# Retrieval scores on one core: the first loads are issued behind single gathers of tile 0

## The reference, cut to what matters

```
retrieved = mean(item_embeddings[indices], axis=1)      # 512 users x 50 indices -> 512 x 512
fused     = concat([user_rep, retrieved], 1) @ W_fuse + b_fuse      # (512 x 1024) @ (1024 x 512)
logits    = fused @ W_proj + b_proj                     # (512 x 512) @ (512 x 12500)
```

## Time and profile before

| What | Value |
|---|---|
| Median of 3 runs | 305.21 us (304.76, 305.21 and 759.52) |
| The profiled execution | 304.97 us, of it the span 303.1 us |
| PE busy | 293.3 us (97%) |
| DVE busy | 241.8 us (80%) |
| ACT busy | 159.4 us (53%) |
| POOL busy | 73.2 us (24%) |
| TensorE's mean granted clock | 0.999 |
| DMA over the span | 75.14 MB, mean 248 GB/s |

### The profile page before, as it was taken

One profiled execution on the slowest core, in us unless ns is written; L12 is line 12 of the kernel. 1 busy time (PEld: TensorE's weight loads), 2 busy tenths in 40 slices (PEclk: granted clock), 3 DMA queues, 4 the chain that ended last, 5 costly groups with the idle time before them and its releaser, 6 DMA issues.

```text
span 303.1 us, 4065 instructions
## 1 busy us (share of the span) xinstructions
PE 293.3 (97%) x1371; PEld 240.0 (79%) x1371; DVE 241.8 (80%) x349; ACT 159.4 (53%) x216; POOL 73.2 (24%) x76
## 2 busy tenths in 40 slices
PE   3999999999999999999999999999999999999995
PEld 1559887978888888888778888888888888888884
DVE  5888999668668699769998979979799797995133
ACT  1205666533544558967465675556855568453310
POOL 4766786777777100000000000000000000000000
PEclk9999999999999999999999999999999999999999
DMA  7999999896997247557875939749397493442315
GB/s 250 363 386 372 402 389 360 297 368 200 333 376 254 71 140 221 185 162 310 292 285 174 352 118 309 286 152 349 123 306 282 143 367 122 152 155 107 128 70 203
DMA packets 32480, 75.14 MB, mean 248 GB/s; under 512 B 4445, under 2 KB 20587, under 8 KB 32460
## 3 DMA queue, kind: packets, MB, share of 16 engines
q1 hardware_dynamic: 25340, 58.31, 54.6%
q0 software_dynamic: 5536, 13.73, 13.2%
q10 hardware_dynamic: 1584, 2.84, 2.5%
HBM read 52.84 MB, written 25.60 MB: 259 GB/s over the span
## 4 chain that ended last, share of the span: by engine, by line
PE 48%; DVE 3%; issue 1%; ACT 0%; DVEq 0%; ACTq 0%
PE pair L1258 16%; PE pair L1256 16%; PE pair L1259 16%; DVE w_lo L962 1%; DVE part_out L987 0%; DVE out_sb L987 0%; DVE w_raw L953 0%; DVE t_sums L945 0%; ACT odd_sum L644 0%; DVE out_sb L1119 0%; DVE t_sums L951 0%; DVE t_sums L957 0%; DVEq L983 0%; DVEq L956 0%; ACTq L639 0%
## 5 line engine op out<-in xcount | busy, mean ns | idle before, releaser
L438 POOL DMA_INDIRECT ring<-item_embeddings,rows x56 | 59.1, 1055 | 19.6 <-issue 15.2
L1256 PE MATMUL pair<-w_hi,s_hi 128*128 128x500 f32 x144 | 56.2, 390 | 0.4 <-ACT odd_sum L644 0.3
L1258 PE MATMUL pair<-w_lo,s_hi 128*128 128x500 f32 x144 | 56.1, 389 | 0.0
L1259 PE MATMUL pair<-w_hi,s_lo 128*128 128x500 f32 x144 | 55.9, 388 | 0.0
L1183 PE MATMUL pair<-w_hi,f_hi 128*128 128x500 f32 x112 | 44.0, 393 | 0.4 <-DVE f_lo L895 0.4
L854 DVE SCALAR_TENSOR_TENSOR pair<-ring,mask,pair 128x512 f32<-128x512 f32 x48 | 36.2, 753 | 9.8 <-DMA ring<-item_embeddings,rows 5.5
L1183 PE MATMUL pair<-w_lo,f_hi 128*128 128x500 f32 x112 | 43.8, 391 | 0.0
L1183 PE MATMUL pair<-w_hi,f_lo 128*128 128x500 f32 x112 | 43.5, 389 | 0.0
L1258 PE MATMUL pair<-w_lo,f_hi 128*128 128x500 f32 x108 | 42.2, 391 | 0.0
L1259 PE MATMUL pair<-w_hi,f_lo 128*128 128x500 f32 x108 | 42.0, 389 | 0.0
L1256 PE MATMUL pair<-w_hi,f_hi 128*128 128x500 f32 x108 | 41.8, 387 | 0.0
(11 more groups left out here) (137 smaller groups left out, 431.2 us busy)
## 6 DMA issues: line engine op xcount, KB each, us to landing
w_raw<-w_proj SPq DMA_DIRECT2D x28, 500.0 KB, 7.5
logits<-part_out SPq DMA_DIRECT2D x24, 500.0 KB, 3.2
early<-w_proj SPq DMA_DIRECT2D x22, 500.0 KB, 5.9
logits<-out_sb SPq DMA_DIRECT2D x23, 250.0 KB, 2.5
logits<-out_sb SPq DMA_DIRECT2D x11, 500.0 KB, 3.2
first_bias<-b_proj SPq DMA_DIRECT2D x10, 250.0 KB, 6.4
s_sum<-b_proj SPq DMA_DIRECT2D x8, 250.0 KB, 7.0
logits<-out_sb ACTq DMA_DIRECT2D x7, 250.0 KB, 7.0
```

Of the source, the lines that this page charges most:

```text
L438: return nc.gpsimd.indirect_dma_start(out=to, out_offset=None, in_=table, in_offset=bass.IndirectOffsetOnAxis(ap=column, axis=0), **how)
L1256: nc.tensor.matmul(ps[:, q, 0:CHUNK], f, hi, start=start and k == 0, stop=False, skip_group_check=True)
L1258: nc.tensor.matmul(ps[:, q, 0:CHUNK], f, lo, start=False, stop=False, skip_group_check=True)
L1259: m = nc.tensor.matmul(ps[:, q, 0:CHUNK], f_rest, hi, start=False, stop=stop and k == 1, skip_group_check=True)
```

## The change

The second half of the user part (k = 2 and 3) is no longer loaded at the start: `user_t[:, 2]` and `wf_user[:, 2]` are issued by SP once slot 0 of tile 0 has landed, those of k = 3 once slot 2 has. ACT now issues only `user_t` of k = 0 and 1. The first half of chunk 0 waits for slot 3, the last row (and the bias rows and `bf_col` behind it) for slot 4, the second half of chunk 0 for slot 5, `wf_ret` for slot 6, chunk 1 for slot 8. `wf_ret` now comes ahead of chunk 1. Chunks 2 to 6 wait for `user_fused` as before, and for slot 8 instead of slot 7.

```diff
-GATE = 7
+USER_BEHIND = (0, 2)
+GATE = 8
...
-            def load_chunk(c):
-                for h in range(2):
+            def load_chunk(c, halves=(0, 1)):
+                for h in halves:
...
             sp.dma_start(idx[:, 0:K], indices[:, 0:K]).then_inc(first_idx_landed, 16)
+            def behind_slot(i):
+                sp.wait_ge(slot_landed[place(0, i)], 16 * slot_uses(0, i))
+
             for k in range(HK):
+                if k >= HK // 2:
+                    behind_slot(USER_BEHIND[k - HK // 2])
+                    sp.dma_start(user_t[:, k, :], user_dram[k]).then_inc(user_landed[k], 16)
                 sp.dma_start(wf_user[:, k, :], wf_dram[0, :, k, :]).then_inc(wf_user_landed[k], 16)
                 if k == 0:
                     sp.dma_start(idx[:, K:TILES * K], indices[:, K:TILES * K]).then_inc(idx_landed, 16)
+            behind_slot(3)
+            load_chunk(0, (0,))
+            behind_slot(4)
             sp.dma_start(last_rows[:], last_item.to_broadcast([P, H])).then_inc(last_landed, 16)
-            load_chunk(0)
             sp.wait_ge(total_zeroed, 1)
             for row in (0, LO_ROW):
                 sp.dma_start(bias_rows[row:row + RESIDENT, :],
                              b_proj[0:RESIDENT * CHUNK].rearrange("(c n) -> c n", n=CHUNK))\
                   .then_inc(bias_rows_landed, 16)
             sp.dma_start(bf_col[:], b_fuse).then_inc(bf_landed, 16)
+            behind_slot(5)
+            load_chunk(0, (1,))
+            behind_slot(6)
+            sp.dma_start(wf_ret[:], wf_dram[1]).then_inc(wf_ret_landed, 16)
+            behind_slot(8)
             load_chunk(1)
-            sp.dma_start(wf_ret[:], wf_dram[1]).then_inc(wf_ret_landed, 16)
             sp.wait_ge(user_fused, 1)
-            sp.wait_ge(slot_landed[place(0, GATE)], 16 * slot_uses(0, GATE))
+            behind_slot(GATE)
             for c in range(2, RESIDENT):
                 load_chunk(c)
...
-            for k in range(HK):
+            for k in range(HK // 2):
                 act.dma_start(user_t[:, k, :], user_dram[k]).then_inc(user_landed[k], 16)
```

## The result

The changed kernel takes 313.76 us (median of 4 runs, 311.88 to 313.84) against 305.25 us: 1.027 times as long, interval 1.022 to 1.0319. The forecast was 307.0 us with a range to 309.6, so it is wrong: the place and the sign are right, the size is 8.5 us instead of 1.8. (One run of the kernel before took 759.52 us and is left out of the ratio.)

The account below looks back on a forecast made before the run. PE, 97% busy, was taken as the bound through its first projection, with DMA transfers close behind. Profiled 304.97 + 2.3 (late chunk 1) - 0.4 (given back) = 306.9, as a median 307.0 us; range 304.4 to 309.6.

Parts of the forecast that it names:

- (a): Engines ahead of slot 0's gather bytes, which start at 6.7 us: 1.0 us with nothing to move.
- (b): From 6.7 to 10.0 us, until bytes of k = 2 come, only gathers run: 1.3 us of DMA time lost.
- (c): After the k = 2 parts, until k = 3 has bytes from 14.5 us: 1.2 us of DMA time lost.
- Faster or unchanged: Rivals: chunk 1 in by 29.4, time 305 (chance 0.22); `wf_user[0]` lands sooner, time 304.2 (chance 0.07).
- Idle DMA time that the waits make: Step on early loads behind SP's waits: 3.5 us of full-rate DMA time lost, none once SP's ring is full.
- The 2.5 us of the earlier trace: A gather in an idle DMA lands 2.5 us after issue; so slot 0 should land at about 7.5.
- Gathers keep their turn: Rival: POOL's gathers keep their share while SP's ring catches up; chunk 1 at 34.2, time 309.4 us; chance 0.17.
- The 0.4 us counted back for `w_lo`: PE's 0.4 us wait for a rest of the weights goes, as DVE is late by less than PE.

Follow-up runs that it names:

- the user waits alone: Kernel before, with only the user parts of k = 2 and 3 held behind slots 0 and 2 and issued by SP: 310.82 us, 1.0191.
- the gathers held: Changed kernel with POOL's gathers of tiles 1 to 3 held until chunk 1 has landed: 311.84 us, 1.0227.
- six kernels of the table: Changed kernel; it without chunk 1's wait, with early user loads, with only slots 3 to 6 waits; the gathers held; the user waits alone: 310.8 to 313.9 us.

## Why the prediction was wrong

**What was right.** PE's first projection decides, and chunk 1, now last, delays it through ACT's order. Slot 0 landed in 3.5 us. The 3.5 us of (a), (b) and (c) were near: from 4 to 15 us the engines moved 254 GB/s, in the kernel before 365, which is 1.22 MB or 3.2 us at 376 GB/s. From 46 us on PE is over 99% busy as before, with no wait over 0.5 us at chunks 2 to 6. Faster or unchanged was never near.

**The step that failed** is the end of *Idle DMA time that the waits make*: "From there on chunk 0, the last row, chunk 0 again and `wf_ret` keep SP's ring full, since slots 3 to 6 come 1.25 us apart and 2.85 MB can't move faster." It put the loss behind 14.5 us at nothing, and the runs show 2.0 us. The window from 15 to 24 us, first in the kernel before, then in the changed kernel, then with the user waits alone:

```profile
15.00:24.00 9.00, 9.00 (x33) 4.82 (x32) 7.93 (x20) 0.61 (x1) 6.23 (x6) 1.00 1.04 368
```

```profile
15.00:24.00 9.00, 8.28 (x31) 4.54 (x30) 7.90 (x19) 0.14 (x1) 6.38 (x6) 1.00 0.95 285
```

```profile
15.00:24.00 9.00, 8.57 (x31) 4.68 (x30) 7.89 (x20) 0.00 (x0) 6.25 (x6) 1.00 0.92 266
```

(368 - 285) x 9 us is 0.75 MB, 2.0 us at 376 GB/s. The later gates are not needed for it. SP waited 0.4 us for slot 4, 2.1 us for slot 6 and not at all for slots 3 and 5, and the kernel with the user waits alone, which has no gate for slots 3 to 6, loses more. SP's ring did not stand empty either: its packets took 38 to 82% of the 16 engines' time in every microsecond of that window. So a ring that has work again does not mean full traffic, and that was the step's premise. Why those packets moved less is open. In all the loss was 5.2 us instead of 3.5 (2.0 more behind 15 us, 0.3 less ahead of it): 1.7 of the miss.

**A row that was read wrongly.** The 2.5 us of the earlier trace rows are not those of a gather like slot 0's. Behind slot 8 of tile 0 the kernel skips indices outside the table, and in the 2.5 us of that gather (71.88 to 74.40) POOL's ring moved 0.04 MB, where a whole slot is 0.262 MB:

```profile
q0 software_dynamic: 167, 0.04, 10.2%
```

The prediction took 2.5 us and a little, some 3.1, for slot 2; it took 5.2, and part k = 3 went out 1.8 us later than forecast. That the sum up to 15 us came out near is in part luck.

**The rival that held as well.** Gathers keep their turn was given 0.17 and set against the forecast as if only one could be true. It added up with it: chunk 1 came 36.1 - 33.4 = 2.7 us behind what the bytes say, the gathers' 1.05 MB account for it, and with the gathers held 0.7 us of it was left. I had rejected the rule for the earlier trace rows's 8.3 us. That row shows that a gather waits long among full rings; it does not show that many gathers together leave the rings to the loads.

**The term that was not in the sum.** The longer `fuse(0)`, 2.43 us: PE stood for 5.98 us, and the granted clock, 1.00 up to 36 us, is 0.59 from 36 to 38 us, while PE stands, and 0.50 from 38 to 42 us, which is 1.2 instead of 2.4 GHz. A forecast of a stall ahead of dense matmuls has to price them at the lower level as well. The Trainium skill (TensorE: Matmul & The Clock Gate, Part 1: The HAM clock gate) describes a gate that lets four of every eight pulses through when PE has not been busy, and the 0.50 of these rows agrees.

Together: the mean at 37.69 instead of 33.4, 4.3 us (1.7 and 2.7, but for rounding), and the clock, 2.4. That is 6.7 us at the first projection (44.08 against 37.4) and 6.8 at the profiled time (313.7 against 306.9).

**Smaller terms.** Part k = 3 was said to land by 17.5; it was issued at 14.21 and held PE until 21.07, 0.72 us. `wf_ret` was due by 29.0 and landed at 20.64 + 12.1 = 32.7, hidden only by the late mean. The second half of chunk 0 was due by 26.2 and was cast at 27.67. The bias rows were due by 21.5 and released ACT's cast at 23.86. The 0.4 us counted back for `w_lo` did not come: PEld waited 0.5 us for it in the changed kernel too, and 0.26 us came back in all.

**Left open.** Why the packets from 15 to 24 us moved less than before at nearly the same share; why `fuse(0)` took between 5.14 and 6.24 us in kernels in which PE stood for similar times; how much of the 8.5 us each single wait of slots 3 to 6 owns.

## What to carry to other kernels

Where the DMA engines are full from the start to the first use of the weights, a wait that holds back an issue costs every byte that did not move meanwhile, and the debt is collected wherever weights are next wanted, whichever engine's order is changed. Do not count on full traffic as soon as the ring has work again: here it was 285 instead of 368 GB/s for 9 us. Count the gathers that run on meanwhile, and let rivals that act at different points add up. Before a landing time is carried over from another transfer, look at the bytes that it moved. Where a stall of some microseconds is forecast ahead of matmuls, price those at the lower clock too.

## What the runs showed of the hardware

- A gather of a whole slot (0.262 MB) landed in 3.5 us where the loads were held back (slots 0 and 1 of the changed kernel), in 4.2 to 5.2 us beside single loads (slots 2 to 5) and in 7.0 to 8.2 us after that (slots 6 to 8); among the full rings of the kernel before, slot 0 took 8.3 us.
- With little but gathers to move (5.5 to 10 us of the changed kernel) the engines moved 133 GB/s at a share of 0.58; slices of 0.75 us show 60 to 262 GB/s, full slices of the same run up to 415.
- The share of busy time does not tell the traffic: from 15 to 24 us 285 GB/s at 0.95 in the changed kernel, 368 GB/s at 1.04 before.
- After PE had stood for 2.50 to 5.98 us (six kernels of the table), `fuse(0)` took 5.14 to 6.24 us instead of 3.81. After 0.46 and 1.28 us it did not change, but in two other runs the 24 matmuls behind a wait of 1.01 and 1.40 us took 4.28 and 4.45 us with the clock down to 0.50, so the length of the wait alone does not tell.
